# Moving the gated linear attention of the third image pair to the other of two woven instruction streams, with its own on-chip buffers

## What is computed

```
h = s4_tokens(x)                            # 256-long kernels of a state space model
h = layernorm(h + causal_attention(h))      # 8 heads            -> X0
h = layernorm(h + L0_ffn(h))                # attention of 32 heads, + residual, then a
                                            # fixed-slot mixture of 8 experts, gelu
h = layernorm(h + gated_linear_attention(h))# 4 heads
h = layernorm(h + L1_ffn(h))                # 8 experts, top 2, relu
```

```
g   = log_sigmoid(x @ Wgk1 @ Wgk2 + b) / 16
S_t = exp(g_t) * S_{t-1} + k_t v_t ;  o_t = q_t S_t * scale        (per head)
o   = rmsnorm(o) * gw * silu(x @ Wg) ;  out = layernorm(x + o @ Wo)
```

## Time and profile before

| | us |
|---|---|
| runs (3), median | 1462.22 (1461.37 to 1464.41) |
| profiled execution, its own time | 1449.68 |
| its span | 1447.9 |
| PE busy in the span | 1081.3 (75%) |
| DVE busy | 681.0 (47%) |
| ACT busy | 488.4 (34%) |
| mean granted TensorE clock | 0.854 of full |

### The profile page before, as it was taken

The page is one execution under the profiler, slowest core; times in us unless marked ns, Lnnn a source line. Parts: engine busy times, 40 slices in busy tenths (PEclk is TensorE's granted clock), DMA queues, the critical chain, the costliest instruction groups (busy, mean ns, idle before and its releaser), DMA issues. The chain is left out here.

```text
span 1447.9 us, 23000 instructions
## 1 busy us (share of the span) xinstructions
PE 1081.3 (75%) x8550; PEld 792.2 (55%) x8550; DVE 681.0 (47%) x1662; ACT 488.4 (34%) x980; POOL 154.8 (11%) x226
## 2 busy tenths in 40 slices
PE   0237978898889798988879986863506999999920
PEld 0124645444664456663547554733506999999910
DVE  7792445664536665457675564153311222222145
ACT  1221323453544442455435552420002333333300
POOL 3870000000000000000000000000071000000053
PEclk9977987888989896999869897975557999999965
DMA  4421020000021000030001200101961111111132
GB/s 126 148 55 53 1 73 15 1 15 1 30 81 30 2 16 15 31 94 1 1 13 44 84 1 15 59 0 50 369 239 53 37 37 39 37 37 38 34 91 91
DMA packets 65612, 78.06 MB, mean 54 GB/s; under 512 B 15089, under 2 KB 57729, under 8 KB 65377
## 3 DMA queue, kind: packets, MB, share of 16 engines
q1 hardware_dynamic: 60592, 62.95, 13.5%
q0 software_dynamic: 4336, 13.50, 2.9%
q10 hardware_dynamic: 576, 0.13, 0.0%
HBM read 55.86 MB, written 20.71 MB: 53 GB/s over the span
## 5 line engine op out<-in xcount | busy, mean ns | idle before, releaser
L1502 DVE TENSOR_REDUCE mx<-scores_ps 128x4 f32<-128x1024 f32 (+1 forms) x160 | 187.0, 1169 | 136.7 <-PE scores_ps L1015 91.8
L1354 ACT ACTIVATE pt<-turned_ps 128x1024 f32<-128x1024 f32 (+1 forms) x160 | 157.9, 987 | 148.3 <-PE turned_ps L1037 102.7
L1949 PEld LDWEIGHTS x_ps<-x_xtT,x_w1s 128*128 128x128 f32 x1248 | 147.6, 194 | 3.5 <-ACT x_xtT L1984 1.6
L1949 PE MATMUL x_ps<-x_xtT,x_w1s 128*128 128x128 f32 x1248 | 148.1, 278 | 1.0 <-ACT x_xtT L1984 1.0
L1961 PE MATMUL x_ps<-x_w,x_hT 128*128 x624 | 141.0, 379 | 0.0
L1961 PEld LDWEIGHTS x_ps<-x_w,x_hT 128*128 128x128 f32 x624 | 115.6, 190 | 14.2
L2100 DVE TENSOR_TENSOR x_y<-x_ps,x_b2b 128x256 f32<-128x256 f32 x39 | 16.6, 425 | 205.4 <-PE x_ps L1961 205.4
L965 POOL COPY vpad<-v 128x64 f32<-128x64 f32 x64 | 17.3, 301 | 734.8 <-PE ps L1076 594.2
L1027 PE MATMUL turned_ps<-q,k 32*128 32x256 f32 x512 | 73.5, 362 | 24.6 <-DVE mx L1502 13.8
L1027 PEld LDWEIGHTS turned_ps<-q,k 32*128 32x128 f32 x512 | 45.7, 209 | 84.0 <-issue 48.5
L1999 ACT ACTIVATE x_hT<-x_ps,x_b1c 128x128 f32<-128x128 f32 x312 | 85.0, 383 | 16.8 <-issue 13.7
(11 more groups left out here) (353 smaller groups left out, 1907.8 us busy)
## 6 DMA issues: line engine op xcount, KB each, us to landing
wexp<-in_L_ffn_w SPq DMA_DIRECT2D x16, 1024.0 KB, 5.3
x_w<-in_L_ffn_W SPq DMA_DIRECT2D x16, 1024.0 KB
x_slots<-s_zero POOLq DMA_DIRECT2D x1, 4992.0 KB, 19.5
x_xt<-x_slots SPq DMA_DIRECT2D x39, 128.0 KB, 2.1
y_slots<-x_y SPq DMA_DIRECT2D x39, 128.0 KB, 1.7
ha<-h SPq DMA_DIRECT2D x16, 256.0 KB, 3.2
x<-hb SPq DMA_DIRECT2D x8, 256.0 KB, 2.3
x_acc<-x SPq DMA_DIRECT2D x4, 512.0 KB, 6.2
```

The lines of the kernel that those rows point to most:

```text
L1354: sc.activation(pt[v.index // 2 % (PT_RING // 2)][:, :, 0:wide], turned_ps[:, :, 0:wide], ACT.Exp)\
L1502: v.tensor_reduce(mx[:, u.group % 2, 0:blocks, u.n:u.n + 2].rearrange("p b n -> p n b"), scores_ps[:, :, 0:blocks * (P if u.causal else T) ...
L1949: last = mm(ps[2 * (i % 2) + f // KH][:, f % KH * P:(f % KH + 1) * P], w1s[:, i % 2, c, f * P:(f + 1) * P], xtT[:, i % 2, c, :], start=c = ...
```

## The change

Y1b of pair 2 is taken out of stream b and put at the end of stream a. There it uses `tt_a`, `yb_a`, `rs_a`, `mv_a`, `stats_a` and new `g4_a`, `qs_a`, `ks_a`, `vg_a`, which are laid over the memory of `nat`, a buffer of Y2. Slots 0 and 1 of Y1b (moments and layer norm that end the feed-forward) become the last two slots of Y1a, so Y1a has 22 slots and Y1b 23, for all pairs. Three needs are added: Y1b of pair 2 after Y1a of pair 2; slot 3 (vg0) of Y1b of pair 3 after slot 18 (p2's transposes) of Y1b of pair 2; slot 21 after slot 22. The semaphores counted per stream follow the side.

```diff
-                 (.9, 0, 0, False, f"down{e}1+1"), (.9, 1, 0, False, "")]],
-        "Y1b": [(0, 3, 0, True, ""), (0, 1.8, 0, True, ""), (.95, .7, .6, True, "h2_t0 h2_t1"),
+                 (.9, 0, 0, False, f"down{e}1+1"), (.9, 1, 0, False, "")]] +
+               [(0, 3, 0, True, ""), (0, 1.8, 0, True, "")],
+        "Y1b": [(.95, .7, .6, True, "h2_t0 h2_t1"),
...
-                   ("Y2s", 2), ("Y2", 3), ("Y2s", 3)),
-             "b": tuple((stage, p) for p in range(PAIRS) for stage in ("Y1a", "Y1b"))}
+                   ("Y2s", 2), ("Y2", 3), ("Y2s", 3), ("Y1b", 2)),
+             "b": (("Y1a", 0), ("Y1b", 0), ("Y1a", 1), ("Y1b", 1), ("Y1a", 2), ("Y1a", 3), ("Y1b", 3))}
...
-            after("Y1b", p - 3, 24, "Y2", p, 6)
+            after("Y1b", p - 3, 22, "Y2", p, 6)
...
+        after("Y1a", 2, 21, "Y1b", 2, 0)
+        after("Y1b", 2, 18, "Y1b", 3, 3)
+        after("Y1b", 2, 22, "Y1b", 3, 21)
...
-    nat = {k: sb("nat_" + k, [P, 2, TOK], f32r) for k in ("q_hi", "q_lo", "k_hi", "k_lo")}
+    natural = ExitStack()
+    nat = {k: sb("nat_" + k, [P, 2, TOK], f32r, natural) for k in ("q_hi", "q_lo", "k_hi", "k_lo")}
+    natural.close()
+    g4_a, qs_a, ks_a, vg_a = sb("g4_a", [P, 4, TOK]), sb("qs_a", [P, TOK]), sb("ks_a", [P, TOK]), sb("vg_a", [P, NTB, D])
...
+    def linear(p):
+        if plan.side("Y1b", p) == "a":
+            return "a", g4_a, qs_a, ks_a, vg_a
+        return "b", g4_b, qs_b, ks_b, vg_b
...
         def y1b(p):
-            for _ in range(2):
-                yield
+            side, g4, qs, ks, vg = linear(p)
+            u1 = qs[0:16, :]
...
-            yield from project(p, "p2", ob, wt.gwo, "b")
+            yield from project(p, "p2", ob, wt.gwo, side)
...
-
-        def y1b(p):
-            h = hb[p % 3]
             moments("b")
             yield
             normalised("b", h, rs["b"][1])
             signal("h2")
             yield
```

More of the change, by code:

```diff
@@ L642, in __init__, with side @@
         self.schedule(work, self.needs(work))
-    def side(self, stage):
-        return "x" if stage in ("X0", "X1") else "a" if stage in ("Y3", "Y2", "Y2s") else "b"
+    def side(self, stage, p):
+        return next((side for side in "ab" if (stage, p) in self.ORDER[side]), "x")
     def needs(self, work):
@@ L652, in after @@
             if (stage, p) in self.start and (then, q) in self.start:
-                needs[self.side(then)][self.start[then, q] + n].append((self.side(stage), self.start[stage, p] + k))
+                needs[self.side(then, q)][self.start[then, q] + n].append((self.side(stage, p), self.start[stage, p] + k))
         for p in range(PAIRS):
@@ L909, in a_stream @@
                     next_ha(stage, p, "h_t1")
+                if stage == "Y1b":
+                    yield from y1b(p)
+                    continue
                 if stage == "Y2":
@@ L1271, in y1b @@
                 last = tr(bank[:, bb * P:(bb + 1) * P], ks[:, 2 * bb * P:(2 * bb + 1) * P], ident[:, :])
[L1272 removed]
+            last.then_inc(sg("y_full_" + side), 1)
             yield
@@ L1281, in y1b @@
                         if tb == NTB - 1:
-                            last.then_inc(sg("y_full_b"), 1)
+                            last.then_inc(sg("y_full_" + side), 1)
                 yield
@@ L1313, in a_stream @@
             for stage, p in plan.ORDER["a"]:
-                yield from {"Y3": y3, "Y2": y2, "Y2s": y2s}[stage](p)
+                yield from {"Y3": y3, "Y2": y2, "Y2s": y2s, "Y1b": y1b}[stage](p)
         def b_stream():
@@ L1433, in y1a @@
                 yield from pause(4)
+            yield from pause(2)
         def y1b(p):
-            yield from pause(2)
-            turned("h2", p, "b")
+            side, g4, qs, ks, vg = linear(p)
+            u1 = qs[0:16, :]
+            gz, gm, ge, gG = (g4[:, i, :] for i in range(4))
+            turned("h2", p, side)
             yield
-            sc.copy(u1[:, :], full("u", p)[0:16, :]).then_inc(sg("y_act_b"), 1)
+            sc.copy(u1[:, :], full("u", p)[0:16, :]).then_inc(sg("y_act_" + side), 1)
             yield from pause(2)
@@ L1686, in y1b @@
             yield
-            turned("h2", p, "b")
+        def y1b(p):
+            side, g4, qs, ks, vg = linear(p)
+            gz, gm, ge, gG = (g4[:, i, :] for i in range(4))
+            h = hb[p % 3]
+            turned("h2", p, side)
             yield
```

126 lines of the change are left out of this document (64 added, 62 removed).

## The result

The changed kernel takes 1440.91 us in the median (4 runs, 1437.4 to 1443.6), the kernel before 1463.32 beside it (4 runs): ratio 0.9842, interval 0.9809 to 0.9875, 22 us less. On another chip the ratio was 0.9906 (0.9873 to 0.9938), on a third 0.9843 (0.9803 to 0.9883). The forecast was 5.6 us less, 1456.6, in a range that ended at 1446. One chip differs from another, and so does one execution of a kernel from the next, so medians are compared only with those measured beside them.

A forecast was written before the change was run, and what follows sets the result against it. TensorE, busy 75% of the span, was taken as the bound, with 28.2 us idle from 814 to 945.5 us to gain. Terms -11.5 + 4.8 - 2.4 - 2.5 + 6.0 = -5.6 us gave 1456.6, range 1446 to 1465.

The forecast's parts named there:

- (f): Earlier pairs: ties between streams a and b go to a; taken as 0, with 3 us either way.
- my opening claim: From 814 to 945.5 us TensorE idles 28.2 us, all there is to gain ahead of Y1b of pair 3.
- (e): Pair 3's feed-forward: pair 2 fills between up fills wait for a bank; four holds at 1.5, +6.0 us (2.6 to 13.6).
- (a): Last head to first up fill of pair 3: projection no longer behind pair 2's p2, 20.8 to 9.3, -11.5 us.
- (b): Pair 2's p2 now runs among pair 3's feed-forward fills: TensorE +4.8 us, its VectorE part hidden.
- (c): Y1b of pair 2 from `at` on, 9.3 us, moves from X1 to the feed-forward, netting zero; a mask wait leaves, -2.4.
- (d): Moved pair 2 work fills holes in pair 3's projection (copy, residual, copy; 3.05 us): -2.5 us.
- (g): SyncE queue: pair 2's layer norm wait could delay pair 3's second expert weights; taken as 0, 3 us kept for upper end.
- more is hidden: Rival: the 5.2 us hole fills, bank holds cost 0.65 each, X1 loses 4 us idle; about -14, 1448; chance 0.16.
- Slower: the banks decide: Rival: full 3.4 us bank holds at pair 3's up fills; five give +5.4, 1467.6 us; chance 0.15.

The follow-up runs named there:

- tail_only: Changed kernel with the order of the kernel before for the first 348 slots, so only the end is changed: 0.9959 to before, again 0.9917.
- after_again: The changed kernel, unchanged, run again: 0.9906 to the kernel before; a third time, on another chip, 1436.22 us, 0.9843.
- p2_behind: Changed streams, order of before through X1's drain; then pair 3's projection and up fills first, pair 2's p2 among the down fills: 0.9971 to before.
- early_only_again: Second run of the kernel before with the changed kernel's order for the first 348 slots, its own order after: 0.9962 to before (first run 0.9965).
- the two halves: Two kernels with the changed end and the changed order in only slots 145 to 187 or only 188 to 348: both 0.9951 to before.
- p2_in_gap: Changed kernel with p2's two product fills of pair 2 moved behind pair 3's last down fill: 0.9855 to before, again 0.9831.

## Why the prediction was wrong

The way was right and the size was not; the term that failed is **(f)**, the order of the earlier pairs, "I take 0, with 3 us either way". I had written just before it that the tails of stream b shrink most and that ties go to a, and then priced it by idle time ("TensorE idles for other reasons too"). Idle time was indeed nearly unchanged, as above. The price lay in the duration of the matmuls: the order changed over 204 of 469 slots, and with it the granted clock. From A to the last head it was 3 to 13 us in the traces; in the medians it was 11 (tail_only to after_again) and 15 (tail_only_again to after_third), by the ratios 8 and 11. My bound left all of that out, and my opening claim, that 28 us of idle behind 814 were all there was to gain, was false for the same reason: it looked neither at the stages ahead of 814 nor at how long the matmuls themselves take.

The other terms, against the end alone (forecast for all but f: 5.6 less; measured 0.9959 and 0.9917, 6 and 12 less). In the traces, from A to the first transposes of hb, tail_only took 539.1 us (328.3 + 153.7 + 14.6 + 42.4), the two profiles of before 542.8 and 546.3: 3.7 and 7.2 less. That this lies round the forecast is luck: (e) was put at +6.0 and was nothing, and (a), (b) and (c) together fell short by about as much.

- **(a) -11.5:** p2_behind shows 20.8 to 12.0, -8.8. The chain is right, but pair 3's product again ran partly at half clock (0.69 granted in that stage) and took 5.87 us, where I took 3.69.
- **(b) +4.8:** the feed-forward grew by 6.9 (35.5 to 42.5) in every kernel that has p2 between the `down` fills; the fills are 5.2 of that (1.34 + 1.89 + 1.97), the rest waits of 0.6 to 1.3.
- **(c) -9.3 and back, -2.4:** X1 ended only 5.4 to 7.1 earlier, since `at` stayed on X1's side. The wait before the second `at` did not leave either, it was 1.47 us in place of 2.39 (in tail_only and in after).
- **(d) -2.5:** right in kind; state and o stand in those holes, and from the last head to the first up fill TensorE is idle 0.8 of 14.7 us.
- **(e) +6.0:** the hold exists, and at 4.0 on average its price is above my upper bound of 3.4. That the wait alone was 3.3 twice is chance: it is made of the eviction of o, one table load and a gelu, not of the two loads and the gelu that I added up, and where those two loads came, the wait was 0.9. The rest is clock, which I had left out here as well. But the order has no hold at all, where I put four. My guess at the planner's filling was wrong: in its table the gap before up03 came when only VectorE's slots of pair 2 were ready. Here the error was towards too small a gain, and cancelled those of (a), (b) and (c).
- **(g)** nothing, as taken: in the feed-forward of pair 3 TensorE never waited for weights.

Of the rivals, "more is hidden" gave 1448 by way of the 5.2 us hole, which did not fill, and of idle time that leaves X1, which it did not. "Slower: the banks decide" had its mechanism right: with three holds the gain of the end is eaten; but the order has no hold. What decided was in none of them.

What stays open: why the new order is granted more clock, since single waits were not moved. Slots 145 to 187 carry 4 to 5 us of the gain in every profile. Why slots 188 to 348 give 6.5 us in one run and take 4 in another is not known. Nor is it known what an execution of the kernel before does that takes as long as its median beside the changed kernel (1463): the two profiled ones took 1449.7 and 1456.4.

## What to carry to other kernels

A static order made by a planner is one object: a change of one stage's stream changes tails, ties and the place of every wait far ahead of it, so look first at where the two orders depart. Idle time is not the whole account of TensorE; compare its busy time at equal instruction counts, because nearly the same waits in other places were worth 3 to 13 us in 480 here. Cut two traces where both orders have issued the same work, or a gain may be work put off. And a fill that takes a shared bank between two others whose evictions are batched can make the next one wait for the whole batch: 3.3 us of wait in two of three here, 4 us each in all.

## What the runs showed of the hardware

The granted clock of a stage that runs alone came out in steps for the same 136 matmuls: 59.5 us (0.70) in five profiles, 61.2 (0.67) in two, and 62.9 to 65.7 (0.60 to 0.66) in eight others, with 21.3 us idle in each of the fifteen (the other three have work of pair 2 in this stage). That alone spreads an unchanged kernel by 6 us, against 0.1 us in the duration of a stage such as up to h2_t (35.5 in both profiles of before).

The second mixture, which no kernel here changes, took 434 to 436 us behind the main loop in the four profiles of one chip (early_only_again, the two halves and p2_in_gap) and 441 to 445 in the other fourteen, for the same 2051 matmuls; TensorE is idle some 127 us in the former (p2_in_gap) and 136 in the latter (after_third). The medians of the kernel before differ accordingly, 1450.4 on that chip and 1458.8 to 1463.3 on the others. Why was not looked into.
